# Moving the cross-attention logits of a batch one iteration later, into another PSUM bank

## The chip, the core and the metric

The kernel runs on one core of one Trainium2 chip. The metric is the device time of one execution in microseconds (us); the execution that the profiler recorded is one more, with a time of its own.

## What is computed

One decoder layer over 16 sequences ("batches") of 100 tokens, width 256: windowed self-attention, cross-attention to 361 context rows with 16 heads, and a mixture of 8 experts of which each token uses 2. Each part ends in residual plus layer norm. What matters here is the seam between the second and the third part:

```python
x = _layernorm(x + attn(x), axis=-1)
x = _layernorm(x + cross_attn(x, ctx_1024, ctx_1024), axis=-1)    # x2
logits = x2.reshape(-1, 256) @ Ws + bs                            # 256 x 8
topk_w, topk_idx = jax.lax.top_k(logits, 2)                       # picks the experts
```

The product `x2 @ Ws` of a batch is a 100 x 8 result. The kernel makes it inside its cross-attention part, batch by batch, and keeps all 16 in the tile `LG`, which only the expert part reads, after all batches.

## The kernel before, in words

Three blocks follow one another: self-attention, cross-attention (`cross_attention`, where the whole change lies) and experts. Every engine has its own in-order instruction stream, written out by hand; engines meet by counting semaphores (`wait_ge(sem, count)`).

Cross-attention is a software pipeline over `i` from -2 to 16. In iteration `i` TensorE works on four batches: it projects keys and queries of `i+2` (`keys`, `queries`), computes scores with queries on the rows and values for `i+1` (`query_scores`, L769; `values`, L839), scores with keys on the rows and weighed values for `i` (`key_scores`, L778; `weigh_values`, L793), and the tail of `i-1`: turning the weighed values, turning the attended rows (`turn_attended`, L854), output projection (`project`, L860), layer norm, turning x2 (`turn_x2`, L867) and the logits (`logits`, L875). The loop over the 16 heads `h` sets the order: every head issues one `query_scores` and one `key_scores`, and the other pieces stand at fixed heads.

VectorE takes one row maximum per head (`maximum`, L1040) from the `query_scores`, and `query_scores(b, h)` waits for the maximum of head h-2. ScalarE takes one exponential per head (`exps`, L937) from the `key_scores`, and `key_scores(b, h)` waits for the exponential of head h-2. ScalarE's other pieces also stand at fixed heads. Those that matter here, in its program order:

- h = 4: `exps`, `keys_out(i+2, 1)` (L948)
- h = 5: `exps`, `second_part(i+2, 0)` (L961, L962)
- h = 6: `exps`, `maximum_out(i, 1)` (L942), `attended_out(i-1)` (L985)
- h = 7: `exps`
- h = 13 to 15: `exps`, `maximum_out(i+1, 0)` (L942); `exps`, `x2T_out(i-1)` (L990); `exps`, `logits_out(i-1)` (L995)

Three PSUM banks are shared by all the odd pieces. M0 holds keys of half 0 and everything of the tail up to x2 turned. M1 holds keys of half 1, the values of the first two chunks (`values(., 0)` and `values(., 1)`) and the turned maximum of half 0. M2 holds queries, the third chunk of values, the turned maximum of half 1, and the logits. A piece that writes a bank waits for the ScalarE or VectorE read of the piece before it in that bank. `keys(b, 0)` waits for `x2T_ev >= b - 3`, which is the x2T copy of the iteration just ended.

Which iterations have which pieces: keys and queries up to i = 13, `query_scores` and values up to i = 14, `key_scores` up to i = 15, the tail from i = 1 to i = 16.

Of the kernel before, what the change touches and what calls it, by code (L numbers as in the profile page):

```python
# [12 lines left out]
ACT = mybir.ActivationFunctionType  # L13
# [3 lines left out]
NB, L, D = 16, 100, 256  # L17
# [31 lines left out]
E, F = 8, 688  # L49
# [31 lines left out]
def wait(eng, sem, count):  # L81

    if not isinstance(count, int) or count > 0:
        eng.wait_ge(sem, count)
# [500 lines left out]
def cross_attention(nc, ps, ident, ctxT, cross, x1d, x1Td, x2d, accd, LG, wg, wu, WG, WU):  # L585
# [9 lines left out]
    with ExitStack() as ctx:  # L595
# [6 lines left out]
        wq_sb, wk_sb, wv_sb, wo_sb, ws_sb = cross.wq, cross.wk, cross.wv, cross.wo, cross.ws  # L602
# [26 lines left out]
        x2T = sb("x2T", [P, KC, L])  # L629
# [15 lines left out]
        mT_ev = [sem(f"mT_ev{u}") for u in range(2)]  # L645

        M0, M1, M2, B_O, B_S, B_T = 0, 1, 2, 3, 4, 6
# [7 lines left out]
        with nc.Block() as block:  # L655
# [99 lines left out]
            def _(pe):  # L755
# [41 lines left out]
                def turn_maximum(b, half):  # L797
                    pe.wait_ge(mxp_ok[half], b + 1)
                    if half == 0:
                        bank = M1  # L800
                        pe.wait_ge(v_ev, 2 * b + 1)
                    else:
                        bank = M2
                        pe.wait_ge(q_ev, min(b + 3, NB))
                        wait(pe, lg_ev, b - 1)
                    pe.matmul(ps[0:SR + MR, bank, 0:L], mxp[:, half, :],
                              negid[:, :], start=True, stop=True).then_inc(mT_mm[half], 1)

# [10 lines left out]

                def queries(b):  # L820
                    pe.wait_ge(x1T_in[b % 2], 16 * (b // 2 + 1))
                    wait(pe, lg_ev, b - 3)
                    for m in range(KC):
                        for k in range(KC):
                            mm = pe.matmul(ps[:, M2, m * L:(m + 1) * L], wq_sb[:, k, m * P:(m + 1) * P],
                                           x1T_sb[b % 2][:, k, :], start=(k == 0), stop=(k == KC - 1))
                    mm.then_inc(q_mm, 1)

                def values(b, c):

                    if c == 0:
                        pe.wait_ge(k_ev, min(2 * b + 4, 2 * NB))
                        wait(pe, mT_ev[0], b)
                    if c == 2:
                        pe.wait_ge(q_ev, min(b + 2, NB))
                        wait(pe, mT_ev[1], b)
                    bank, o = (M1, c * D) if c < 2 else (M2, 0)
                    for k in range(KC):
                        mm = pe.matmul(ps[0:CM, bank, o:o + D], cx[b % NX][:, k, c * CH:c * CH + CM], wv_sb[:, k, :],  # L839
                                       start=(k == 0), stop=(k == KC - 1))  # L840
                    if c > 0:
                        mm.then_inc(v_mm, 1)
# [8 lines left out]
                def turn_attended(b):  # L851
                    pe.wait_ge(at_ok, b + 1)
                    for k in range(KC):
                        mm = pe.transpose(ps[:, M0, k * L:(k + 1) * L], at[:, k * P:(k + 1) * P], ident[0:L, 0:L])  # L854
                    mm.then_inc(aT_mm, 1)
# [13 lines left out]

                def logits(b):  # L870
                    pe.wait_ge(x2T_ev, b + 1)
                    pe.wait_ge(v_ev, min(2 * b + 6, 2 * NB))
                    pe.wait_ge(mT_ev[1], min(b + 2, NB))
                    for k in range(KC):
                        mm = pe.matmul(ps[0:L, M2, 0:E], x2T[:, k, :], ws_sb[:, k, :],  # L875
                                       start=(k == 0), stop=(k == KC - 1))
                    mm.then_inc(lg_mm, 1)

                for i in ITER:
                    kq, s, t, tail = stages(i)  # L880
                    if kq and not t:
                        wait(pe, k_ev, 2 * (i + 2))
                        wait(pe, q_ev, i + 2)
                        keys(i + 2, 0)
                        queries(i + 2)
                        keys(i + 2, 1)
                    for h in range(H):
                        if s:
                            query_scores(i + 1, h)
                        if t:  # L890
                            key_scores(i, h)
                        if h == 0 and kq and t:
                            keys(i + 2, 0)
                        if h == 1 and kq and t:
                            queries(i + 2)
                        if h == 2 and tail:
                            weigh_values(i - 1, NG - 1)
                        if h == 3 and kq and t:
                            keys(i + 2, 1)
                        if h == 4 and tail:  # L900
                            turn_weighed(i - 1)
                        if h == 4 and t:
                            turn_maximum(i, 1)
                        if h == 5 and t:
                            weigh_values(i, 0)
                        if h == 6 and tail:
                            turn_attended(i - 1)
                        if h == 7 and s:
                            values(i + 1, 0)
                        if h == 8 and tail:  # L910
                            project(i - 1)
                        if h == 9 and t:
                            weigh_values(i, 1)
                        if h == 10 and s:
                            values(i + 1, 1)
                        if h == 11 and s:
                            values(i + 1, 2)
                        if h == 12 and s:
                            turn_maximum(i + 1, 0)
                        if h == 13 and t:  # L920
                            weigh_values(i, 2)
                        if h == 14 and tail:
                            turn_x2(i - 1)
                        if h == 15 and tail:
                            logits(i - 1)

            @block.scalar
            def _(act):
# [54 lines left out]
                def attended_out(b):  # L983
                    act.wait_ge(aT_mm, b + 1)
                    act.activation(atT[:, :, :], ps[:, M0, 0:KC * L].rearrange("p (k l) -> p k l", k=KC),  # L985
                                   ACT.Copy).then_inc(aT_ev, 1)

                def x2T_out(b):
                    act.wait_ge(x2T_mm, b + 1)
                    act.activation(x2T[:, :, :], ps[:, M0, 0:KC * L].rearrange("p (k l) -> p k l", k=KC),  # L990
                                   ACT.Copy).then_inc(x2T_ev, 1)

                def logits_out(b):
                    act.wait_ge(lg_mm, b + 1)
                    act.activation(LG[:, b:b + 1, :], ps[0:L, M2, 0:E].unsqueeze(1), ACT.Copy).then_inc(lg_ev, 1)  # L995

                for i in ITER:
                    kq, s, t, tail = stages(i)
                    for h in range(H):
                        if t:  # L1000
                            exps(i, h)
                        if h == 0 and kq:
                            keys_out(i + 2, 0)
                        if h == 1 and kq:
                            queries_out(i + 2)
                        if h == 2 and tail:
                            weighed_out(i - 1)
                        if h == 4 and kq:
                            keys_out(i + 2, 1)
                        if h == 5 and kq:  # L1010
                            second_part(i + 2, 0)
                        if h == 6 and t:
                            maximum_out(i, 1)
                        if h == 6 and tail:
                            attended_out(i - 1)
                        if h == 9 and kq:
                            second_part(i + 2, 1)
                        if h == 11 and s:
                            values_out(i + 1, 0)
                        if h == 12 and s:  # L1020
                            values_out(i + 1, 2)
                        if h == 13 and s:
                            maximum_out(i + 1, 0)
                        if h == 14 and tail:
                            x2T_out(i - 1)
                        if h == 15 and tail:
                            logits_out(i - 1)

            @block.vector
# [612 lines left out]
```

## Time and profile before

| what | value |
|---|---|
| median of 3 runs | 768.74 us (766.88 to 768.89) |
| the profiled execution | 764.9 us, span of its core 763.1 us |
| mean granted TensorE clock | 0.926 of full speed |
| TensorE matmul busy over the span | 653.7 us (86%) |
| VectorE, ScalarE, GpSimd busy | 380.3, 318.8, 260.2 us |
| cross-attention's steady iterations | from about 168 us to 400 us of the span |

Times count from the start of the span. "PE" is TensorE's matmuls, "PEld" its weight loads, DVE is VectorE, ACT is ScalarE. A line such as L875 is the line of the instruction in the kernel; a bracket at the end of a timeline row is the idle time of the engine ahead of it and what released it. Matmul ends are modelled, so starts are the better marker on TensorE. ScalarE's instructions overlap a little: the next starts some 0.1 us before the recorded end of the one before.

### The profile page before, as it was taken

To read this page: it belongs to the slowest core of one execution; us is meant where nothing else is said; L and a number is where in the kernel's file an instruction comes from. 1 tells how busy PE (TensorE), PEld (TensorE's weight loads), DVE (VectorE), ACT (ScalarE), POOL (GpSimd) and SP (SyncE) were. 2 spreads that over 40 slices of the span, in tenths; PEclk is the share of its full clock that TensorE was granted. 3 is DMA by queue.
4 is the path that set the end of the run, shared out by engine and by line. 5 is a ranking of instruction groups with operands and counts; after the bars stand their busy time and mean duration, and the time that the engine had idled before them with its cause. 6 is when DMAs were issued, how large, how long until landed. Compare 5 with 4: busy or idle time off the path is not lost. (4 is left out here: it accounts for less than half of the span.)

```text
span 763.1 us, 15406 instructions
## 1 busy us (share of the span) xinstructions
PE 653.7 (86%) x5196; PEld 516.8 (68%) x5197; DVE 380.3 (50%) x898; ACT 318.8 (42%) x757; POOL 260.2 (34%) x461
## 2 busy tenths in 40 slices
PE   6989845599999999999998426999999999999960
PEld 5888733277777777777777326777777777777740
DVE  3787742667777777777775290222222222222213
ACT  2434412277777767777776200222222222212204
POOL 4253442234433343343341201233433433433223
PEclk9999957699999999999999755999999999999995
DMA  8231112545655555655555170021111211121105
GB/s 253 80 75 45 55 46 56 138 111 158 189 160 156 154 166 155 177 156 160 156 140 158 43 310 14 22 39 26 30 34 27 34 33 27 28 34 27 20 9 163
DMA packets 61145, 73.72 MB, mean 97 GB/s; under 512 B 7768, under 2 KB 52128, under 8 KB 60320
## 3 DMA queue, kind: packets, MB, share of 16 engines
q1 hardware_dynamic: 54944, 65.48, 29.2%
q0 software_dynamic: 6144, 7.48, 5.9%
q8 instruction: 35, 0.57, 0.3%
q14 instruction: 22, 0.18, 0.1%
HBM read 38.25 MB, written 12.39 MB: 66 GB/s over the span
## 5 line engine op out<-in xcount | busy, mean ns | idle before, releaser
L1040 DVE TENSOR_REDUCE cmx<-ps 100x1 f32<-100x361 f32 x256 | 133.6, 532 | 67.4 <-PE ps L769 65.3
L937 ACT ACTIVATE cpr<-ps 121x300 f32<-121x300 f32 x256 | 105.0, 420 | 52.6 <-PE ps L778 51.9
L1532 DVE TENSOR_TENSOR hh<-sg,ps 128x344 f32<-128x344 f32 x64 | 32.8, 513 | 131.9 <-PE ps L1342 131.9
L769 PE MATMUL ps<-st 96*100 96x361 bf16 x256 | 85.5, 337 | 13.6 <-DVE cmx L1040 8.5
L778 PEld LDWEIGHTS ps<-st 120*121 120x121 bf16 x768 | 81.4, 136 | 20.0 <-issue 5.4
L1280 POOL DMA_INDIRECT accd<-y,si x32 | 51.3, 1603 | 124.1 <-DVE y L1543 124.1
L1364 PE MATMUL ps<-WD,hT 128*128 x384 | 88.3, 380 | 1.3 <-ACT hT L1408 1.3
L1342 PE MATMUL ps<-WG,xsT 128*128 x256 | 86.0, 459 | 0.6 <-ACT xsT L1397 0.6
L1342 PE MATMUL ps<-WU,xsT 128*128 x256 | 85.2, 455 | 0.0
L778 PE MATMUL ps<-st 120*121 120x100 bf16 x768 | 82.3, 216 | 2.4 <-ACT st L942 1.5
L1364 PEld LDWEIGHTS ps<-WD,hT 128*128 128x128 f32 x384 | 72.8, 190 | 16.0 <-issue 1.8
L1397 ACT ACTIVATE xsT<-ps 128x256 f32<-128x256 f32 x32 | 12.3, 383 | 136.0 <-PE ps L1330 136.0
L729 POOL COPY parts<-parts 128x722 bf16<-128x722 bf16 x32 | 29.4, 919 | 115.1 <-DVE parts L1047 115.1
L1342 PEld LDWEIGHTS ps<-WU,xsT 128*128 128x128 f32 x256 | 49.2, 192 | 25.9 <-issue 1.0
L769 PEld LDWEIGHTS ps<-st 96*100 96x100 bf16 x256 | 32.2, 126 | 32.6 <-DVE cmx L1040 20.3
L1342 PEld LDWEIGHTS ps<-WG,xsT 128*128 128x128 f32 x256 | 44.3, 193 | 14.2 <-issue 1.4
L839 PE MATMUL ps<-cwv_sb,cx 128*121 128x256 f32 x192 | 52.9, 399 | 0.0
L1404 ACT ACTIVATE sg<-ps 128x344 f32<-128x344 f32 x64 | 29.2, 457 | 55.1 <-PE ps L1342 55.1
L1543 DVE TENSOR_SCALAR y<-ps,wt 128x256 f32<-128x256 f32 x32 | 15.5, 484 | 71.0 <-PE ps L1364 71.0
L816 PE MATMUL ps<-cx,cwk_sb 128*128 128x361 f32 x128 | 47.5, 494 | 1.2 <-ACT kf L948 0.7
L793 PE MATMUL ps<-cpr,cva 120*32 120x100 f32 (+1 forms) x1536 | 46.4, 253 | 0.0
L1269 POOL DMA_INDIRECT xs<-x2d,gi x32 | 32.4, 1012 | 25.5 <-POOL gi L1266 25.5
(189 smaller groups left out, 1077.2 us busy)
## 6 DMA issues: line engine op xcount, KB each, us to landing
st<-parts SPq DMA_DIRECT2D x192, 115.2 KB, 2.4
WD<-in_wd SPq DMA_DIRECT2D x6, 1024.0 KB, 10.4
cx<-in_ctxT SPq DMA_DIRECT2D x16, 361.0 KB, 5.2
WG<-in_wg SPq DMA_DIRECT2D x8, 688.0 KB, 4.9
WU<-in_wu SPq DMA_DIRECT2D x8, 688.0 KB, 4.7
x_sb<-in_x SPq DMA_DIRECT2D x8, 200.0 KB
x1d<-x SPq DMA_DIRECT2D x8, 200.0 KB
x1Td<-x1T SPq DMA_DIRECT2D x8, 200.0 KB, 2.9
```

Source lines behind the costliest of these rows:

```text
L769: pe.matmul(ps[0:L, B_S + h % 2, 0:CTX], st[b % NX][0:SR, h, CTX:KQ], st[b % NX][0:SR, h, 0:CTX], start=True, stop=True).then_inc(s_mm, 1)
L778: mm = pe.matmul(ps[0:CM, B_T + h % 2, c * L:(c + 1) * L], st[b % NX][:, h, c * CH:c * CH + CM], st[b % NX][:, h, CTX:KQ], start=True, sto ...
L793: mm = pe.matmul(ps[j * VC:(j + 1) * VC, B_O, g * L:(g + 1) * L], va[b % 2][0:n, c, h, :], pr[0:n, h % (2 * HG), c * L:(c + 1) * L], start ...
L816: mm = pe.matmul(ps[:, M0 + m, 0:CTX], wk_sb[:, k, m * P:(m + 1) * P], cx[b % NX][:, k, :], start=(k == 0), stop=(k == KC - 1))
L839: mm = pe.matmul(ps[0:CM, bank, o:o + D], cx[b % NX][:, k, c * CH:c * CH + CM], wv_sb[:, k, :], start=(k == 0), stop=(k == KC - 1))
L937: act.activation(pr[:, h % (2 * HG), :], ps[0:CM, B_T + h % 2, 0:NCH * L], ACT.Exp).then_inc(exp_ok, 1)
L1040: dve.tensor_reduce(mx[:, half, hh:hh + 1], ps[0:L, B_S + h % 2, 0:CTX], AX_X, ALU.max).then_inc(max_ok, 1)
L1269: pool.indirect_dma_start(xs[:, t.par, :], None, x2d, bass.IndirectOffsetOnAxis(ap=gi[:, t.par:t.par + 1], axis=0))\
L1280: pool.indirect_dma_start(accd, bass.IndirectOffsetOnAxis(ap=si[:, t.par:t.par + 1], axis=0), y[:, t.par, :], None, compute_op=ALU.add, bo ...
L1342: mm = pe.matmul(ps[:, bank + f, 0:FH], xsT[:, t.par, k, :], W[:, k, bass.ds(e, 1), f * FH:(f + 1) * FH], start=(k == 0), stop=(k == KC - 1))
L1364: mm = pe.matmul(ps[:, B_Y, 0:D], hT[:, t.par, c, :], WD[:, c, bass.ds(e, 1), :], start=(c == 0), stop=(c == FC - 1))
L1532: dve.tensor_tensor(hh[:, t.par, f * FH:(f + 1) * FH], sg[:, f, :], ps[:, B_U + f, 0:FH], ALU.mult).then_inc(h_ok, 1)
```

## The change

The logits of batch `b` were made at head 15 of iteration `b+1`, right behind the x2 that they need, in bank M2. Now they are made at head 6 of iteration `b+2`, in bank M1, between the keys of half 1 and the first values; ScalarE's copy of them to `LG` stands at head 7 of that iteration. The last batch stays at head 15 of iteration 16. The waits follow: `queries` and `turn_maximum(., 1)` no longer wait for the copy, `values(., 0)` does, and the x2T copy of the next batch waits for the logits matmuls of this one.

```diff
                     else:
                         bank = M2
                         pe.wait_ge(q_ev, min(b + 3, NB))
-                        wait(pe, lg_ev, b - 1)
...
                 def queries(b):
                     pe.wait_ge(x1T_in[b % 2], 16 * (b // 2 + 1))
-                    wait(pe, lg_ev, b - 3)
...
                     if c == 0:
                         pe.wait_ge(k_ev, min(2 * b + 4, 2 * NB))
                         wait(pe, mT_ev[0], b)
+                        wait(pe, lg_ev, b - 2)
...
                 def logits(b):
                     pe.wait_ge(x2T_ev, b + 1)
-                    pe.wait_ge(v_ev, min(2 * b + 6, 2 * NB))
-                    pe.wait_ge(mT_ev[1], min(b + 2, NB))
+                    pe.wait_ge(k_ev, min(2 * b + 10, 2 * NB))
+                    pe.wait_ge(mT_ev[0], min(b + 3, NB))
                     for k in range(KC):
-                        mm = pe.matmul(ps[0:L, M2, 0:E], x2T[:, k, :], ws_sb[:, k, :],
+                        mm = pe.matmul(ps[0:L, M1, 0:E], x2T[:, k, :], ws_sb[:, k, :],
...
+                        if h == 6 and i >= 2:
+                            logits(i - 2)
                         if h == 7 and s:
                             values(i + 1, 0)
...
-                        if h == 15 and tail:
+                        if h == 15 and i == NB:
                             logits(i - 1)
...
                 def x2T_out(b):
                     act.wait_ge(x2T_mm, b + 1)
+                    wait(act, lg_mm, b)
...
                 def logits_out(b):
                     act.wait_ge(lg_mm, b + 1)
-                    act.activation(LG[:, b:b + 1, :], ps[0:L, M2, 0:E].unsqueeze(1), ACT.Copy).then_inc(lg_ev, 1)
+                    act.activation(LG[:, b:b + 1, :], ps[0:L, M1, 0:E].unsqueeze(1), ACT.Copy).then_inc(lg_ev, 1)
...
                         if h == 6 and tail:
                             attended_out(i - 1)
+                        if h == 7 and i >= 2:
+                            logits_out(i - 2)
...
-                        if h == 15 and tail:
+                        if h == 15 and i == NB:
                             logits_out(i - 1)
```

At head 6 the logits stand behind `turn_attended(i - 1)`; at head 7 of ScalarE `logits_out` stands behind that head's exponential.

## Rows read from the trace of the kernel before

**Rows 1.** The page's first line.

```profile
span 763.1 us, 15406 instructions
```

**Rows 2.** Stretches: busy PE, PEld, DVE, ACT, POOL; granted clock, DMA share, GB/s.

```profile
310.00:328.00 18.00, 17.37 (x208) 14.00 (x209) 13.41 (x30) 13.03 (x33) 6.81 (x17) 1.00 0.57 160
418.00:420.00 2.00, 0.98 (x22) 0.72 (x11) 0.09 (x1) 1.42 (x4) 0.00 (x0) 1.00 0.59 231
432.00:434.00 2.00, 0.59 (x2) 0.29 (x2) 0.41 (x1) 0.26 (x1) 0.56 (x1) 0.50 0.05 11
```

**Rows 3.** TensorE's waits from 150 to 450 us: total, times, longest.

```profile
PE ps L875 <- ACT x2T L990: 9.7, 16, 0.6
```

**Rows 4.** Timeline of ScalarE: the logits copies of i = 1 and 13.

```profile
185.62 0.18 ACT L995 ACTIVATE LG<-ps 100x8 f32<-100x8 f32 x1 [0.29 <-PE ps L875]
...
399.76 0.18 ACT L995 ACTIVATE LG<-ps 100x8 f32<-100x8 f32 x1 [0.29 <-PE ps L875]
```

**Rows 5.** Timeline of TensorE, i = 8, heads 6 to 8.

```profile
300.45 0.39 PE L854 MATMUL ps<-ident,at 100*128 100x100 f32 x2
300.68 0.32 PE L769 MATMUL ps<-st 96*100 96x361 bf16 x1
300.84 0.32 PE L778 MATMUL ps<-st 120*121 120x100 bf16 x3
300.99 1.09 PE L839 MATMUL ps<-cwv_sb,cx 128*121 128x256 f32 x4
...
302.35 1.11 PE L860 MATMUL ps<-cwo_sb,atT 128*100 128x256 f32 x4
```

**Rows 6.** Timeline of ScalarE, i = 8, heads 4 to 9.

```profile
298.59 0.42 ACT L937 ACTIVATE cpr<-ps 121x300 f32<-121x300 f32 x1 [1.18 <-PE ps L778]
...
300.67 0.41 ACT L937 ACTIVATE cpr<-ps 121x300 f32<-121x300 f32 x1
301.10 0.84 ACT L942 ACTIVATE st<-ps 24x800 bf16<-24x800 f32 x1
301.96 0.34 ACT L985 ACTIVATE atT<-ps 128x200 f32<-128x200 f32 x1
302.19 0.73 ACT L937 ACTIVATE cpr<-ps 121x300 f32<-121x300 f32 x2
303.81 0.42 ACT L937 ACTIVATE cpr<-ps 121x300 f32<-121x300 f32 x1 [0.89 <-PE ps L778]
```

**Rows 7.** Timeline of TensorE around the end of i = 8.

```profile
309.03 0.32 PE L778 MATMUL ps<-st 120*121 120x100 bf16 x3
309.98 0.52 PE L875 MATMUL ps<-ws_sb,x2T 128*100 128x8 f32 x4 [0.63 <-ACT x2T L990]
310.36 0.34 PE L769 MATMUL ps<-st 96*100 96x361 bf16 x1
310.53 0.32 PE L778 MATMUL ps<-st 120*121 120x100 bf16 x3
310.69 1.44 PE L816 MATMUL ps<-cx,cwk_sb 128*128 128x361 f32 x4
```

**Rows 8.** Timeline of ScalarE in the same place.

```profile
309.28 0.42 ACT L937 ACTIVATE cpr<-ps 121x300 f32<-121x300 f32 x1
309.60 0.33 ACT L990 ACTIVATE x2T<-ps 128x200 f32<-128x200 f32 x1
```

**Rows 9.** Timeline of VectorE in the same place.

```profile
308.72 1.04 DVE L1040 TENSOR_REDUCE cmx<-ps 100x1 f32<-100x361 f32 x2 [0.20 <-PE ps L769]
```

**Rows 10.** Timeline of TensorE, i = 14, heads 7 and 8.

```profile
404.98 1.09 PE L839 MATMUL ps<-cwv_sb,cx 128*121 128x256 f32 x4
...
406.22 1.07 PE L860 MATMUL ps<-cwo_sb,atT 128*100 128x256 f32 x4
```

**Rows 11.** Timeline of TensorE, i = 15 and 16, heads 6 to 15.

```profile
419.88 0.37 PE L778 MATMUL ps<-st 120*121 120x100 bf16 x3 [1.02 <-ACT st L942]
...
429.41 1.11 PE L860 MATMUL ps<-cwo_sb,atT 128*100 128x256 f32 x4 [0.43 <-ACT atT L985]
```

## The prediction

> **What bounds the kernel now.** I read first the page's first line, which gives the span that the sum is made against [rows 1]: 763.1 us, in an execution that took 764.9 us. Then the busy time by stretch. In an 18 us stretch of steady cross-attention TensorE is busy 17.37 us, VectorE 13.41, ScalarE 13.03, at a granted clock of 1.00 [rows 2]. So TensorE sets the pace there, and whatever is put on or taken off its stream changes the time one to one, until another engine's chain catches up locally. The copies of the logits come at 185.62 us (i = 1) and 399.76 us (i = 13) [rows 4], twelve iterations apart: (399.76 - 185.62) / 12 = 17.845 us per iteration, so that one iteration (i = 8) can stand for i = 2 to 13. Next, TensorE's waits: its largest repeated one is for the x2T copy ahead of the logits, 9.7 us over 16 times [rows 3], 0.63 us in a steady iteration [rows 7]. That is the wait that the change takes the logits away from. Last, the timelines of TensorE and ScalarE at head 15 (where the logits leave) and at heads 6 to 8 (where they arrive).
>
> **Part A: what the logits leave behind at head 15.** Before, at the end of i = 8, the last key scores start at 309.03, then TensorE waits for x2T and starts the logits at 309.98, query scores of the next head 0 follow at 310.36, key scores at 310.53, keys at 310.69 [rows 7]. The logits themselves thus hold the stream for 310.36 - 309.98 = 0.38 us. Without them the order is key scores, query scores, key scores, keys. What holds each:
> - query scores of head 0 need the maximum of head 14: the pair of maxima starts at 308.72 and takes 1.04 us, so the first ends near 309.24 [rows 9];
> - key scores of head 0 need the exponential of head 14: 309.28 + 0.42 = 309.70 [rows 8], and with 0.05 us for the signal 309.75 (x2T ends at 309.60 + 0.33 = 309.93, the logits start at 309.98 [rows 7, 8]: that is 0.05 us from a ScalarE end to a TensorE start);
> - keys follow 0.16 us behind (310.69 - 310.53), at 309.91, but `keys(i+2, 0)` writes the bank from which x2T is read and waits for the same copy. So keys start at 309.98.
>
> So the stall isn't removed; two short pieces move into it, and it now ends at the keys instead of the logits. Keys move from 310.69 to 309.98, a gain of 0.71 us, for the twelve iterations i = 1 to 12 that are followed by one with keys: 8.5 us. For i = 13, 14 and 15 there are no keys behind, but the exponentials of heads 14 and 15 hold the key scores instead; no row prices that, so I bound it by nothing and by 0.71 us each and take half, 0.35 us: 1.05 us. Part A: -9.6 us. Its bounds: -5.7 us (only the logits' own 0.38 us, 15 times) and -10.65 us (0.71 us, 15 times).
>
> **Part B: what arrives at heads 6 and 7.** The logits go behind the turned attended rows, which start at 300.45. Query scores of head 7 move from 300.68 to 301.06, key scores from 300.84 to 301.22, and values could start at 300.99 + 0.38 = 301.37 [rows 5]. But they have a new wait: the copy of the logits. ScalarE has that behind the exponential of head 7, and is late there. It starts head 6's exponential at 300.67, then spends 0.84 us on the maximum (301.10) and 0.34 us on the attended rows (301.96), and head 7's exponential starts only at 302.19 [rows 6]. With the recorded steps of ScalarE (the next starts about 0.1 us before the end of the last: 301.96 + 0.34 = 302.30 against 302.19 [rows 6]) the copy starts at 302.19 + 0.42 - 0.11 = 302.50, takes 0.18 us [rows 4], and ends at 302.68. With 0.05 us for the signal the values start at 302.73. That is 302.73 - 300.99 = 1.74 us later than before, of which 0.38 us is the logits and 1.36 us is TensorE standing idle. In TensorE's stream everything from there on is queued behind it: head 8's scores, the projection, all of the rest of the iteration; VectorE's maxima and ScalarE's exponentials wait for those.
>
> ScalarE can't come earlier: at head 4 it was itself waiting for TensorE, 1.18 us, until 298.59 [rows 6]. So its lateness isn't inherited but made afresh in each iteration, by the 302.68 - 298.59 = 4.1 us of work from head 4 to the copy, against 301.37 - 298.59 = 2.8 us to the values. A shift of the iteration as a whole moves both.
>
> A little comes back. Before, the projection waits for the attended rows (302.30 + 0.05 = 302.35) and starts 302.35 - 300.99 = 1.36 us behind the values [rows 5, 6]; in i = 14, where it doesn't have to wait, it starts 406.22 - 404.98 = 1.24 us behind them [rows 10]. After the change it never has to. That gives 0.12 us: 1.74 - 0.12 = 1.62 us per iteration. From there on ScalarE was already waiting for TensorE before (0.89 us at 303.81 [rows 6]), so nothing more is recovered.
>
> The wait binds from i = 2 (in i = 1 its count is zero) to i = 14 (the last with values): 13 x 1.62 = +21.1 us. Bounds: a copy that starts at once and needs no signal gives 1.5 us (19.5 us), nothing recovered and 0.05 us more for the copy 1.8 us (23.4 us).
>
> **Part C: the rest.** In i = 15 the logits lie in front of a wait of 1.02 us for the maximum [rows 11] and cost nothing; in i = 16 TensorE waits 0.43 us for the attended rows right behind the place [rows 11]. The new wait of the x2T copy for the logits matmuls is met about eight heads earlier. The two waits taken from `queries` and `turn_maximum` never ended last: TensorE's waits show no row for them. SP, GpSimd and all DMAs have the same instructions as before; their queues have more time per iteration, not less. If that cover failed it would show at head 0 or 8 as a wait for the stacked tile. The last batch is untouched, so the hand-over to the experts only shifts. Part C: 0.
>
> **The sum.** -9.6 + 21.1 + 0 = +11.5 us. On the profiled execution: 763.1 + 11.5 = 774.6 us of span, 764.9 + 11.5 = 776.4 us. The median of the three runs lies 3.8 us above the profiled execution, for which I have no cause in the rows; the change's own runs will lie around the median, so I forecast 768.7 + 11.5 = 780.2 us, slower by 1.5%.
>
> **The clock, beside the sum.** TensorE is granted 1.00 in the steady stretches with their 0.63 us of waiting, and still 1.00 in a 2 us stretch where it is busy only 0.98 us and waits 1.02 us in one piece; it is at 0.50 in a later one with 0.59 us busy [rows 2, 11]. A new idle of 1.36 us, once in some 18.7 us, is nearer to the first two. The Trainium skill ("TensorE: Matmul & The Clock Gate", section "A second HAM failure mode: psum-queue depth-cycling") speaks against this change: frequent small idles of TensorE as it cycles through PSUM banks can make its clock swing between full and half speed. By that rule the time would be that of the second rival below; the trace so far doesn't agree, since the clock stays at 1.00 through the idles shown.
>
> **The rivals.**
> 1. *The copy is in time; faster.* Place: `values(i+1, 0)` at head 7. If ScalarE's copy ended before TensorE got there, the cost of part B would be the logits' 0.38 us, 13 times 4.9 us, and the total 4.9 - 9.6 = -4.7 us: 764.0 us. It decides where the new idle is 0.36 us or less (13 x 0.36 = 4.7). For it: ScalarE's busy share is only 13.03 of 18 us [rows 2]. Against: the timeline puts it 1.36 us late, in each of the 13 iterations. Chance 0.04.
> 2. *The clock falls behind the new idle.* If values and projection (1.09 and 1.11 us [rows 5]) ran at half speed behind it, each iteration would lose 2.2 us more, 28.6 us in all: 808.8 us. Chance 0.04.
> 3. *The loss is given back.* ScalarE and VectorE are ahead after the new idle; if some later wait of TensorE that I read as its own pace were in truth theirs, most of the 11.5 us could return: about 769 us. Against: ScalarE waits for TensorE right behind. Chance 0.03.
> 4. *Part A gives only its lower bound.* The head 0 pieces are held longer than I read, and 0.38 us is all that is won: 768.7 + 21.1 - 5.7 = 784.1 us. Chance 0.07.
>
> **How the numbers follow.** My forecast has 0.82. From the bounds: 19.5 - 10.65 = +8.9 us and 23.4 - 5.7 = +17.7 us, so 777.6 to 786.4 us on the median; with the runs' own scatter downward (766.88 is 1.9 us below the median) the range is 775 to 787 us. It takes in rival 4, and leaves out 1 to 3 and the odd miss, under 2 in 10. A difference of 0.3% (2.3 us) is about what these runs can tell from none. Faster has 0.04 (rival 1), the same 0.03 (rival 3), slower 0.93.
>
> **What would show it.** In the profile after: the iteration takes 17.845 - 0.71 + 1.62 = 18.76 us; TensorE's waits have a new row, the values' matmul for the copy of the logits, 13 times 1.36 us, 17.7 us together; the x2T wait is now in front of the keys, about 12 times, some 0.1 to 0.3 us as TensorE sees it; values start about 0.05 us after the copy ends; the granted clock stays at 1.00. I would be wrong if the copy stood ahead of head 7's exponential in time, if a wait for the stacked tile or the maxima appeared, or if the clock fell.

## The result and the profile after

The changed kernel takes 801.85 us (median of 4 runs, 799.91 to 802.5) against 768.82 us (4 runs, 766.88 to 769.29) before: ratio 1.0423, 95% interval 1.0403 to 1.0444. That is +33 us, where +11.5 us and at most 787 us were forecast. The direction is right, the size is not, and the time lies outside the range.

The page's first lines of the changed kernel:

```profile
span 800.7 us, 15409 instructions
## 1 busy us (share of the span) xinstructions
PE 680.1 (85%) x5196; PEld 533.8 (67%) x5197; DVE 377.2 (47%) x898; ACT 319.2 (40%) x757; POOL 256.5 (32%) x461
```

The count of matmuls is what it was, 5196, and yet TensorE is busy 680.1 us in place of 653.7 us. The same work took 26 us longer: a hint of the clock before any stretch is looked at. TensorE's waits from 150 to 480 us (total, times, longest):

```profile
PE ps L838 <- ACT LG L997: 17.5, 13, 1.4
...
PE ps L874 <- ACT x2T L992: 0.4, 1, 0.4
```

The wait of [rows 3] has gone from the logits except for the last batch, and the new one stands where it was forecast: 13 times, 17.5 us (17.7 us forecast). Timeline of TensorE in i = 8, heads 6 to 8, to be read against [rows 5]:

```profile
318.18 0.39 PE L853 MATMUL ps<-ident,at 100*128 100x100 f32 x2
318.41 0.44 PE L874 MATMUL ps<-ws_sb,x2T 128*100 128x8 f32 x4
318.71 0.34 PE L769 MATMUL ps<-st 96*100 96x361 bf16 x1
318.88 0.32 PE L778 MATMUL ps<-st 120*121 120x100 bf16 x3
320.56 2.03 PE L838 MATMUL ps<-cwv_sb,cx 128*121 128x256 f32 x4 [1.36 <-ACT LG L997]
```

and of ScalarE in the same place, against [rows 6]:

```profile
318.40 0.41 ACT L938 ACTIVATE cpr<-ps 121x300 f32<-121x300 f32 x1
318.84 0.84 ACT L943 ACTIVATE st<-ps 24x800 bf16<-24x800 f32 x1
319.70 0.34 ACT L986 ACTIVATE atT<-ps 128x200 f32<-128x200 f32 x1
319.93 0.41 ACT L938 ACTIVATE cpr<-ps 121x300 f32<-121x300 f32 x1
320.23 0.18 ACT L997 ACTIVATE LG<-ps 100x8 f32<-100x8 f32 x1
```

ScalarE goes through the maximum's copy, the attended rows and head 7's exponential before it comes to the logits, and TensorE idles 1.36 us. That this is the forecast figure to the hundredth is luck: the bracket counts from the modelled end of the key scores (318.88 + 0.32 = 319.20), while the forecast counted from the start that the values could have had, 0.15 us behind the start of the key scores [rows 5]. Counted so, the idle is 320.56 - 319.03 = 1.53 us. What was not forecast is the 2.03 us of the four value matmuls behind it: in [rows 5] they take 1.09 us. One-microsecond stretches of the changed kernel around that idle (length, busy times of PE, PEld, DVE, ACT, POOL, then the granted clock, DMA share, GB/s):

```profile
318.00:319.00 1.00, 1.00 (x14) 0.87 (x12) 1.00 (x4) 0.98 (x4) 0.00 (x0) 1.00 0.52 165
319.00:320.00 1.00, 0.20 (x4) 0.07 (x2) 1.00 (x4) 0.98 (x3) 0.00 (x0) 1.00 0.02 6
320.00:321.00 1.00, 0.44 (x1) 0.47 (x2) 0.00 (x0) 0.42 (x3) 0.94 (x2) 0.77 0.41 110
321.00:322.00 1.00, 1.00 (x4) 0.69 (x4) 0.00 (x0) 0.00 (x0) 0.78 (x5) 0.50 0.57 154
322.00:323.00 1.00, 1.00 (x7) 0.70 (x5) 0.07 (x1) 0.00 (x0) 0.10 (x1) 0.50 0.74 202
323.00:324.00 1.00, 1.00 (x5) 0.73 (x5) 1.00 (x2) 0.42 (x1) 0.00 (x0) 0.52 0.49 125
324.00:325.00 1.00, 1.00 (x19) 0.78 (x21) 0.28 (x2) 0.11 (x1) 0.00 (x0) 1.00 0.45 124
```

The granted clock falls from 1.00 to 0.50 (from 2.4 to 1.2 GHz) as TensorE comes back from the idle, and is back at 1.00 from 324 us on. Values, scores and projection are done at half speed. The logits copies of i = 3 and i = 13:

```profile
217.28 0.18 ACT L997 ACTIVATE LG<-ps 100x8 f32<-100x8 f32 x1
...
422.82 0.18 ACT L997 ACTIVATE LG<-ps 100x8 f32<-100x8 f32 x1
```

(422.82 - 217.28) / 10 = 20.55 us per iteration, against 17.845 us [rows 4] and a forecast of 18.76 us.

The other end of the change, head 15, is nearly as forecast. TensorE's timeline there (end of i = 7, against [rows 7]) and ScalarE's (against [rows 8]):

```profile
309.52 0.32 PE L778 MATMUL ps<-st 120*121 120x100 bf16 x3
309.90 0.33 PE L769 MATMUL ps<-st 96*100 96x361 bf16 x1
310.34 0.34 PE L778 MATMUL ps<-st 120*121 120x100 bf16 x3
310.57 1.45 PE L815 MATMUL ps<-cx,cwk_sb 128*128 128x361 f32 x4
```

```profile
309.78 0.42 ACT L938 ACTIVATE cpr<-ps 121x300 f32<-121x300 f32 x1
310.10 0.33 ACT L992 ACTIVATE x2T<-ps 128x200 f32<-128x200 f32 x1
```

Scores of head 0 now stand inside the stall, held one after the other, and the keys start 310.57 - 310.10 = 0.47 us behind the start of the x2T copy, against 310.69 - 309.60 = 1.09 us before [rows 7, 8]. The list of waits has no row for the keys: they start 0.23 us behind the key scores, where the step without a wait is 0.16 us [rows 7], so 0.07 us of the stall is left there and the rest lies ahead of the two scores.

**Where the 37.6 us between the two profiled spans are.** By the starts of the projection of i = 1 (177.44 and 179.31 us), of the first values of i = 14 (404.98 [rows 10] and 440.23 us) and of the last logits copy (435.00 and 471.66 us): 1.9 us lie ahead of anything that the change touches; 33.4 us between the first two marks, in i = 1 to 14; 1.4 us from there to the last copy; 0.9 us behind it. The first and last of these are within the scatter between executions (the 17 runs of the kernel before on one chip below go from 765.25 to 771.6 us). So nearly the whole question is the steady iterations.

### The profile page after: what moved, and what is told of

Its sections match the earlier page's. It is cut to its first block and busy times, and to the rows that moved or that the text cites. A ratio compares the mean times of both kernels' runs of the same rounds, so it can differ in the third digit from the quotient of the medians.

```text
span 800.7 us, 15409 instructions
## 1 busy us (share of the span) xinstructions
PE 680.1 (85%) x5196; PEld 533.8 (67%) x5197; DVE 377.2 (47%) x898; ACT 319.2 (40%) x757; POOL 256.5 (32%) x461
## 5 line engine op out<-in xcount | busy, mean ns | idle before, releaser
L778 PEld LDWEIGHTS ps<-st 120*121 120x121 bf16 x768 | 83.8, 140 | 26.5 <-issue 12.8
L769 PE MATMUL ps<-st 96*100 96x361 bf16 x256 | 88.2, 348 | 14.0 <-DVE cmx L1044 8.3
L778 PE MATMUL ps<-st 120*121 120x100 bf16 x768 | 85.1, 221 | 3.9 <-ACT st L943 1.2
L838 PE MATMUL ps<-cwv_sb,cx 128*121 128x256 f32 x192 | 62.2, 454 | 17.5 <-ACT LG L997 17.5
L838 PEld LDWEIGHTS ps<-cwv_sb,cx 128*121 128x121 f32 x192 | 36.4, 210 | 23.2 <-issue 18.7
```

The costliest lines, as they stand in the source:

```text
L769: pe.matmul(ps[0:L, B_S + h % 2, 0:CTX], st[b % NX][0:SR, h, CTX:KQ], st[b % NX][0:SR, h, 0:CTX], start=True, stop=True).then_inc(s_mm, 1)
L778: mm = pe.matmul(ps[0:CM, B_T + h % 2, c * L:(c + 1) * L], st[b % NX][:, h, c * CH:c * CH + CM], st[b % NX][:, h, CTX:KQ], start=True, sto ...
```

## The experiments

Times are medians. Each kernel is set against runs of the kernel before on the same chip; kernels that name the same time and number of runs of it share them. In an iteration "with a loss" the clock falls behind the idle, seen by four value matmuls that take more than 1.13 us.

### Filling the idle with work: six matmuls, and three

```diff
                         wait(pe, mT_ev[0], b)
+                        if b > 2:
+                            for _ in range(6):        # 3 in the second kernel
+                                pe.matmul(ps[:, B_O, 400:512], ident[:, :], ident[:, 0:112], start=True, stop=True)
                         wait(pe, lg_ev, b - 2)
```

> The changed kernel, with six fp32 matmuls of 112 columns (operands: the identity, result in unused columns of the bank of the weighed values) issued by TensorE ahead of the values' new wait, in the 13 iterations that have it; they should fill about 1.15 of the 1.36 us that TensorE otherwise idles. Theory (clock): what the changed kernel lost beyond 11.5 us is TensorE's clock falling behind the idle; with the idle filled the clock stays at 1.00, iterations take 18.76 us, and the time is about 780 us. Rival (contention): values and projection are slow because of the transfers that run at the same time or because of the bank; then filling changes nothing: 802 us, iterations of 20.5 us.

> The same with three such matmuls, so that about 0.75 us of idle is left, near the 0.63 us that the kernel before had at head 15 at full clock. Theory (clock, falls only behind a long idle): 780 us, clock 1.00. Rival (any idle at this place is enough): clock falls again, about 802 us. Contention: 802 us.

Six: 782.46 us (778.77 to 784.96), before 768.81 us (17 runs), ratio 1.0189 (1.0157 to 1.0221). Three: 779.7 us (778.36 to 780.63), ratio 1.0159 (1.0129 to 1.0189). TensorE in the kernel with six, then in the kernel with three:

```profile
347.10 1.55 PE L834 MATMUL ps<-ident 128*128 128x112 f32 x12
348.52 1.13 PE L841 MATMUL ps<-cwv_sb,cx 128*121 128x256 f32 x4
```

```profile
345.64 0.89 PE L834 MATMUL ps<-ident 128*128 128x112 f32 x6
347.06 1.13 PE L841 MATMUL ps<-cwv_sb,cx 128*121 128x256 f32 x4 [0.54 <-ACT LG L1000]
```

The values start no sooner (they still wait for the copy) and nothing else is changed, transfers and bank included, but they take 1.13 us and the clock is 1.00 in every stretch from 200 to 380 us. More work on TensorE, 22 us less time with three (801.85 - 779.7), 19 us with six. The theory of the clock stands and that of contention falls. The kernel with three is also the measurement of my sum without the clock: its copies stand at 214.85 and 403.40 us, (403.40 - 214.85) / 10 = 18.86 us per iteration (18.76 forecast), and 779.7 - 768.8 = +10.9 us in all (+11.5 forecast).

### The copy of the logits moved forward on ScalarE

```diff
                         if h == 6 and t:
                             maximum_out(i, 1)
+                        if h == 6 and i >= 2:
+                            logits_out(i - 2)
                         if h == 6 and tail:
                             attended_out(i - 1)
-                        if h == 7 and i >= 2:
-                            logits_out(i - 2)
```

> The changed kernel, with ScalarE's copy of the logits at head 6 between the maximum's copy and the attended rows, in place of head 7. The copy should end 0.67 us sooner, near 302.0 on the time axis of the kernel before, the idle be about 0.7 us, and the delay per iteration 0.95 in place of 1.62 us. Theory: clock stays at 1.00, 13 x 0.95 - 9.6 = +2.8 us, about 771.5 us. If the clock falls all the same: about 22 us more, 793 us.

775.4 us (772.91 to 777.7), ratio 1.0102 (1.0072 to 1.0131). The idle is 0.82 us, the clock stays at 1.00, and iterations take 18.38 us where 17.845 + 0.95 - 0.71 = 18.09 us was expected: the mechanism holds. Of the 0.29 us, 0.18 us are the two signals taken too short (below), and 0.11 us is the copy's start: it stands behind the maximum's copy (323.92 + 0.84 = 324.76) and starts at 324.78, with none of the overlap that I counted on.

Next, the logits matmuls at head 5 of TensorE and their copy ahead of the maximum's:

```diff
 # TensorE
                         if h == 5 and t:
                             weigh_values(i, 0)
+                        if h == 5 and i >= 2:
+                            logits(i - 2)
...
-                        if h == 6 and i >= 2:
-                            logits(i - 2)
...
 # ScalarE
+                        if h == 6 and i >= 2:
+                            logits_out(i - 2)
                         if h == 6 and t:
                             maximum_out(i, 1)
...
-                        if h == 7 and i >= 2:
-                            logits_out(i - 2)
```

> The changed kernel, with the logits matmuls at head 5 behind the weighed values of group 0 and their copy at head 6 ahead of the maximum's copy, so that the copy ends before TensorE comes to the values. Theory: no wait at the values, the clock at 1.00, cost per iteration 0.38 - 0.12 = 0.26 us, 3.4 us in all, against 9.6 us won at head 15: -6.2 us, about 763 us. Rival (the x2T wait's end at the keys gives nothing): 768.8 + 3.4 - 5.7 = 766.5 us. Clock falls even so: 785 us or more.

766.29 us (12 runs, 764.36 to 771.66), ratio 0.9983 (0.9961 to 1.0005): the whole loss is gone, and what is left can't be told from the kernel before. TensorE still waits 2.1 us in 13 pieces of up to 0.2 us for the copy, iterations take 17.58 us. Its time is that of the rival in my expectation (766.5 us), but not by the rival's mechanism: with only 0.38 us won at head 15 an iteration would take 17.845 + 0.26 - 0.38 = 17.72 us. The wait of 0.17 us, which neither side counted (13 x 0.17 = 2.2 us), is most of what keeps the time above the 763 us of my theory.

### The same idle in the kernel before, without the change

```diff
                         wait(pe, mT_ev[0], b)
+                        if b > 2:
+                            pe.wait_ge(exp_ok, H * (b - 1) + 8)
```

> The kernel before, with nothing moved: the first values of iterations 2 to 14 alone wait, for the exponential of head 7 that the kernel has anyway. TensorE should idle about 1.45 us there, the values start 1.64 us later net, 13 times 21.3 us. Theory (the clock falls behind an idle of 1.36 us or more, whatever bank or logits have to do with it): another 12 x 1.74 = 21 us, iterations near 21.2 us, and 811 us in all. Rival (the fall comes from the logits or their bank): clock stays at 1.00, about 790 us, iterations of 19.5 us.

802.59 us (799.7 to 803.44), before 769.98 us (12 runs), ratio 1.0441 (1.0404 to 1.0479). Two of its 13 idles on TensorE (i = 3 and 5), alike in length and in their place in the iteration:

```profile
216.03 1.10 PE L841 MATMUL ps<-cwv_sb,cx 128*121 128x256 f32 x4 [1.60 <-ACT cpr L939]
...
256.61 2.03 PE L841 MATMUL ps<-cwv_sb,cx 128*121 128x256 f32 x4 [1.60 <-ACT cpr L939]
```

The fall needs neither the logits nor their bank: an idle alone does it. But my expectation of 811 us was too high, because only 7 of the 12 idles of 1.60 us have a loss (iterations 19.46 us without, 21.12 us with; the thirteenth, in i = 14, is 1.44 us and passes), while in the changed kernel all 12 shorter ones of 1.35 to 1.36 us have (its thirteenth, of 1.20 us, passes). With seven the sum comes out: 12 x (19.46 - 17.845) + 7 x 1.66 = 31 us, measured 32.6 us. So the length of an idle is not all that decides.

### One filling matmul: an idle of 0.98 us

The diff is that of the first experiment with `range(1)`.

> The changed kernel with one filling matmul ahead of the values' wait, so that about 1.08 us of idle is left, between the 0.54 us left by three (clock stayed) and 1.36 us by none (clock fell). The changed kernel's iteration 14 idled 1.20 us without losing its clock. If the length of the idle decides and 1.08 us is short enough: iterations of 18.86 us and about 780 us. If it isn't: about 802 us.

Neither: 792.46 us, single runs of 781.13, 791.86, 793.07 and 794.49 us, before 769.98 us. The four lie too far apart for one ratio to stand for them. Values of i = 6, 7 and 8 in the profiled execution:

```profile
271.55 1.12 PE L841 MATMUL ps<-cwv_sb,cx 128*121 128x256 f32 x4 [0.99 <-ACT LG L1000]
...
290.40 1.54 PE L841 MATMUL ps<-cwv_sb,cx 128*121 128x256 f32 x4 [0.99 <-ACT LG L1000]
310.93 1.59 PE L841 MATMUL ps<-cwv_sb,cx 128*121 128x256 f32 x4 [0.99 <-ACT LG L1000]
```

Idles of one length: i = 2 to 6 pass without a loss, 18.86 us apart, and from i = 7 to 13 every one has a loss, 20.52 us apart (310.93 - 290.40 = 20.53); that of i = 14 is 0.83 us and passes. Once it begins it goes on. An iteration with a loss is 1.66 us longer and seems to bring the next idle to an equally bad moment.

### The idle in two pieces: the first values behind head 8's scores

```diff
-                        if h == 7 and s:
+                        if h == 8 and s:
                             values(i + 1, 0)
                         if h == 8 and tail:
                             project(i - 1)
```

> The changed kernel with the first values at head 8, behind that head's scores, in place of head 7; logits and copy as in the change. The idle is then broken in two by 0.31 us of scores. Theory: both pieces are under 0.75 us, the clock stays at 1.00, and the 0.31 us of scores are done inside the wait: iterations of 18.55 us, 13 x 0.31 = 4 us under the filled run's 779.7 us, about 775.7 us. If the sum of idle within a stretch decides and not its pieces: the clock falls, about 797 us.

783.2 us (6 runs, 776.08 to 786.83), before 769.98 us, ratio 1.0189 (1.015 to 1.0227). The profiled execution is the fastest (776.08 us, iterations 18.56 us, as expected), and in it one of 13 (i = 6) has a loss, with 0.46 us of idle ahead of the values and 0.37 us ahead of head 8's key scores:

```profile
270.47 1.68 PE L838 MATMUL ps<-cwv_sb,cx 128*121 128x256 f32 x4 [0.46 <-ACT LG L997]
```

The others, 7 us longer in the median, have granted clocks of 0.909 to 0.924 against 0.926; I have no trace of them, so that they lost the clock oftener is argued, not shown. My expectation that pieces under 0.75 us keep the clock does not hold.

### Longer iterations with the same idle, and the changed kernel again

```diff
+                        if h == 12 and s and i >= 2:
+                            for _ in range(2):
+                                pe.matmul(ps[:, B_O, 400:512], ident[:, :], ident[:, 0:112], start=True, stop=True)
                         if h == 12 and s:
                             turn_maximum(i + 1, 0)
```

> The changed kernel with two of the filling matmuls put at head 12 of iterations 2 to 14, far from the idle, which stays at 1.36 us ahead of the values. They lengthen each iteration by about 0.56 us. Theory (an idle of this length costs the clock only when it comes at some moments, and an iteration of 20.5 us brings it back at the same moment each time, so that the changed kernel loses it in 12 of 12): with iterations of 19.4 us without and 21.1 us with a loss, as in the run with the idle alone, only about 7 of 13 lose it, 779.7 + 7.3 + 7 x 1.7 = 799 us, under the changed kernel although TensorE has more to do. Rival (the length of the idle alone decides): 12 of 13 lose it, 779.7 + 7.3 + 22 = 809 us.

> The changed kernel itself once more, on the same chip as the run beside it. 801.9 us, iterations of 20.5 us, 12 of 13 idles with a loss of clock.

Longer: 801.08 us (800.42 to 802.9), ratio 1.0424 (1.0377 to 1.0472). Again: 801.54 us (799.25 to 802.38), ratio 1.0419 (1.037 to 1.0468); before 767.74 us. The repeat has its loss in 12 of 13 idles and iterations of 20.5 us, like the first. In the longer one, values of i = 3, 4 and 5:

```profile
217.43 2.03 PE L838 MATMUL ps<-cwv_sb,cx 128*121 128x256 f32 x4 [1.35 <-ACT LG L1000]
238.21 1.10 PE L838 MATMUL ps<-cwv_sb,cx 128*121 128x256 f32 x4 [1.35 <-ACT LG L1000]
257.39 1.23 PE L838 MATMUL ps<-cwv_sb,cx 128*121 128x256 f32 x4 [1.36 <-ACT LG L1000]
```

Ten of 13 have a loss (ten of the twelve of 1.35 us; that of i = 14 is 1.19 us and passes), neither the seven of my theory nor the twelve of the rival. In i = 4 (and again in i = 9) the same idle of 1.35 us passes without one, and the time is that of the changed kernel although the filling adds 19.18 - 18.86 = 0.32 us to each iteration, 4 us in all: two losses fewer. It speaks for the theory that the moment counts, but weakly: one more run at another length would be needed to call the repetition at 20.5 us shown.

### A version that beats both

The kernel with logits at head 5, and the copy one step earlier still on ScalarE:

```diff
                     for h in range(H):
+                        if h == 6 and i >= 2:
+                            logits_out(i - 2)
                         if t:
                             exps(i, h)
...
-                        if h == 6 and i >= 2:
-                            logits_out(i - 2)
                         if h == 6 and t:
                             maximum_out(i, 1)
```

> As the run with logits at head 5, and their copy one step earlier still, ahead of head 6's exponential. It should take away the 0.17 us that the values still wait in 13 iterations: iterations of 17.41 in place of 17.58 us and 2.2 us less, about 764 us, clock at 1.00. Rival: the copy then holds up the exponential and the maximum's copy, the projection waits for the attended rows again, and nothing is won: 766 us.

763.18 us (7 runs, 761.94 to 765.01), before 769.98 us, ratio 0.993 (0.9905 to 0.9955). Its copies of i = 3 and 13:

```profile
212.65 0.17 ACT L997 ACTIVATE LG<-ps 100x8 f32<-100x8 f32 x1
...
386.98 0.17 ACT L997 ACTIVATE LG<-ps 100x8 f32<-100x8 f32 x1
```

(386.98 - 212.65) / 10 = 17.43 us per iteration (17.41 expected), no wait at the values, the clock at 1.00. So the change of place and bank is worth 6.8 us, 0.7%, once the copy is ahead of the work that made ScalarE late.

## Why the prediction was wrong

**What bounds, and part A.** Right in what holds each piece: the stall did not go, the two scores moved into it, and it ends at the keys. The gain at head 15 is 1.09 - 0.47 = 0.62 us (0.71 forecast). Of the wait for x2T that was to show ahead of the keys, 0.1 to 0.3 us about 12 times, only some 0.07 us is left, and the profile lists none. The term that was too good is the signal: 0.05 us, taken from one place. Head 14's exponential ends at 309.78 + 0.42 = 310.20 and the scores that wait for it start at 310.34, 0.14 us later.

**Part B.** Right in place, count and, nearly, size. The idle is there 13 times. From the keys of half 1 (296.79 before, 314.53 after) to the values it is 320.56 - 314.53 = 6.03 us against 4.20 us, +1.83 us (1.74 forecast): 0.30 us for the logits (318.71 - 318.41; 0.38 forecast) and 1.53 us of idle counted as the forecast counted it (1.36). Again the signal was too short, 320.56 - 320.41 = 0.15 us, and the shorter logits hide part of that. At full clock the projection then comes 1.25 us behind the values (i = 14 of the changed kernel: 440.23 and 441.48 us), against 1.36 us, so 0.11 us come back (0.12 forecast). By these pieces an iteration should be 1.83 - 0.11 - 0.62 = 1.10 us longer; measured at full clock it is 18.86 - 17.845 = 1.01 us. Most of the last 0.1 us is the filling's own doing: in the kernel with three the values start 347.06 - (346.83 + 0.18) = 0.05 us behind the copy, not 0.15 us, and 347.06 - 341.13 = 5.93 us behind the keys, not 6.03 us.

**Part C.** Right for head 6 of i = 15, where the wait behind the logits is 0.70 us in place of 1.02 us. Behind that it missed something. At the end of i = 15 TensorE no longer has the logits to do and idles ahead of the last weighed values; the changed kernel, then the granted clock there:

```profile
460.40 1.20 PE L793 MATMUL ps<-cpr,cva 120*32 120x100 f32 x24 [0.70 <-ACT cpr L938]
```

```profile
460.00:462.00 2.00, 1.20 (x24) 0.84 (x24) 0.00 (x0) 0.69 (x3) 0.00 (x0) 0.62 0.27 89
```

From there to the last copy it takes 471.66 - 460.40 = 11.26 us, before 435.00 - 425.79 = 9.21 us, with the lower clock. But the version that beats both and the kernel with three filling matmuls have this 0.70 us too and keep their clock there, so it is not certain in every execution.

**The step that failed** is "The clock, beside the sum": "A new idle of 1.36 us, once in some 18.7 us, is nearer to the first two" (the 0.63 us of the steady stretches and the 1.02 us of i = 15, both at 1.00). From two idles that passed I drew that a longer one would pass, and gave the fall 0.04. What the runs showed in its place: the clock falls behind 12 of the 13 idles, an iteration with a loss takes 20.55 - 18.86 = 1.7 us more, 12 x 1.7 = 20 us, and the lower clock at the end of i = 15 adds 11.26 - 9.21 = 2 us in the profiled execution. With the 10.9 us of the kernel with three filling matmuls that makes 33 us, the result. It is my second rival, whose time of 808.8 us (2.2 us a loss, 13 times) was 7 us too high: the clock is already back at the end of the projection, and i = 14 is spared. Its mechanism and price were in the text; its chance and so the range were wrong.

The trace of the kernel before had more to say, in its self-attention part, which I did not read for this. TensorE idles there six times, 11.3 us apart, and once more behind the last; then two stretches, read as in [rows 2]:

```profile
34.92 0.55 PE L328 MATMUL ps<-ident,pr 100*100 100x100 f32 x4 [1.18 <-ACT pr L419]
...
91.34 0.55 PE L328 MATMUL ps<-ident,pr 100*100 100x100 f32 x4 [1.07 <-ACT pr L419]
92.76 2.62 PE L338 MATMUL ps<-va,prT 100*100 100x65 f32 x16 [0.87 <-ACT prT L394]
```

```profile
34.00:92.00 58.00, 51.55 (x424) 47.27 (x424) 45.66 (x130) 25.66 (x64) 26.25 (x26) 1.00 0.24 61
93.00:94.00 1.00, 1.00 (x9) 1.00 (x9) 0.00 (x0) 0.00 (x0) 0.00 (x0) 0.57 0.04 11
```

Five idles of 1.07 to 1.18 us passed at a clock of 1.00; behind the sixth and the one of 0.87 us that follows it the clock fell to 0.50. So an idle of over a microsecond had passed several times, and yet the clock had also been lost behind idles shorter than the new one. None of these rows could exclude the fall, and the range should have reached to it. What decides which idle is followed by a fall stays open.

The rule that I set against the sum there, of the Trainium skill ("TensorE: Matmul & The Clock Gate", section "A second HAM failure mode: psum-queue depth-cycling"), that small frequent idles of TensorE, as it cycles through PSUM banks, can make its clock swing between full and half speed, agrees with the trace after, with 1.00 and 0.50 in the stretches above. The run with the idle alone shows that it takes no change of bank. I weighed the rule against rows that were too few.

**The other rivals.** The first (copy in time, -4.7 us) is what the last experiment builds, at -6.8 us; the change itself doesn't meet its condition. The third and the fourth didn't occur.

## What to carry to other kernels

When a move of work puts a wait of around a microsecond in front of a TensorE that was busy without a break, price it twice, once as time and once at half clock for what comes behind, and give the second a real chance. Idles as long that passed in the trace are no proof: here 1.07 to 1.18 us passed five times in the kernel before, and 0.98 us cost the clock seven times in the kernel with one filling matmul. Before moving a piece, look up what its consumer's engine has queued ahead at the new place: here a copy of 0.18 us stood behind three other pieces of ScalarE (the maximum's copy, the attended rows, head 7's exponential) and left TensorE idle for over a microsecond. With the logits one head earlier and that copy ahead of head 6's exponential, +33 us became -7 us.

## What was not expected of the hardware

The same idle costs the clock at one time and not at another. In the profiled executions 7 of 12 idles of 1.60 us had a loss, all 12 of 1.35 to 1.36 us in the changed kernel (both times), 10 of 12 of that length in longer iterations, 7 of 12 of 0.98 us (the runs of that kernel go from 781 to 794 us), one of 13 pairs of up to 0.37 and 0.46 us, and none of those of 0.54 and 0.82 us. With a loss in each, iterations settled at 20.5 us in three profiled executions of two kernels and stayed there until i = 14, whose idle is shorter; and useless work on TensorE, put into the idle, made the program 22 us shorter.
